# Constants and scalar parameters of a gate stage moved into the stage before it, and its first products reordered

## The reference

```python
# per head and chunk of 32: T = inverse of a unit lower triangle, then
u = T @ (v * beta);  w = T @ (k * beta)
def step(S, (q_i, k_i, u_i, w_i)):                   # over the chunks
    attn = where(incl_lower, q_i @ k_i.T, 0)
    u_adj = u_i - w_i @ S
    o_i = q_i @ S + attn @ u_adj
    S = S + k_i.T @ u_adj
local_short = fir(v, 3 taps);  local_long = fir(v, 63 taps)
stats = [mean, var, mean |x|, l2 norm] of local_short, local_long, delta_out, v
logits = gelu([hs, stats] @ gW1 + gb1) @ gW2 + gb2
probs = softmax(logits / exp(log_temp))
floor = 0.05 * sigmoid(floor_param)
probs = probs * (1 - sum(floor)) + floor
o = probs[0] * local_short + probs[1] * local_long + probs[2] * delta_out + probs[3] * v
o = o + sigmoid(conv_res_logit) * local_short + alpha_id * (hs @ Wid)
o = rms_norm(o) * o_norm_w;  out = o @ Wo             # then norm and routing to one of 8 experts
```

## Time and profile before

| | |
|---|---|
| Time, median of 3 runs | 1134.49 us (1133.34 to 1134.78) |
| The profiled execution's own time | 1135.28 us |
| Its span, first to last instruction | 1133.1 us |
| Mean granted clock of PE | 0.873 |
| PE busy | 909.3 us (80%) |
| DVE busy | 739.6 us (65%) |
| ACT busy | 556.5 us (49%) |
| POOL busy | 459.8 us (41%) |
| Inverse stage, from PE's first transposes | 678.0 us on |
| Gate stage, opening | 744.7 to 789 us |
| Gate stage, loop | 789 to about 1006 us |

### The profile page before, as it was taken

One profiled execution on the slowest core, in us unless ns is written; L12 is line 12 of the kernel. 1 busy time (PEld: TensorE's weight loads), 2 busy tenths in 40 slices (PEclk: granted clock), 3 DMA queues, 4 the chain that ended last, 5 costly groups with the idle time before them and its releaser, 6 DMA issues. The chain is left out here.

```text
span 1133.1 us, 34126 instructions
## 1 busy us (share of the span) xinstructions
PE 909.3 (80%) x12733; PEld 648.5 (57%) x12734; DVE 739.6 (65%) x2236; ACT 556.5 (49%) x1120; POOL 459.8 (41%) x590
## 2 busy tenths in 40 slices
PE   5899999999724999992788979479998996308995
PEld 2466666676613998992344447366555542307884
DVE  3558888888452555551488888913788888624664
ACT  1466766666311555551566753154455545206773
POOL 1001333444462444442477620021135555544776
PEclk8799999999656999997799979767999888658998
DMA  2011211245012222213333230131112151011210
GB/s 89 20 40 48 58 39 49 59 124 160 23 42 62 61 60 56 56 54 95 83 89 86 43 117 39 75 108 53 49 54 64 59 197 39 19 38 47 53 54 21
DMA packets 122117, 73.15 MB, mean 65 GB/s; under 512 B 63363, under 2 KB 108521, under 8 KB 121600
## 3 DMA queue, kind: packets, MB, share of 16 engines
q1 hardware_dynamic: 115328, 58.59, 18.9%
q0 software_dynamic: 6656, 12.70, 3.5%
HBM read 42.69 MB, written 27.51 MB: 62 GB/s over the span
## 5 line engine op out<-in xcount | busy, mean ns | idle before, releaser
L1129 ACT ACTIVATE bx_h<-bx_up,bx_cur 128x128 f32<-128x128 f32 x288 | 82.1, 368 | 104.4 <-PE bx_up L1100 104.4
L577 POOL DMA_INDIRECT regions_b<-a_xo,a_seat x64 | 63.7, 996 | 132.7 <-DVE a_seat L872 115.6
L1058 POOL DMA_INDIRECT chosen_b<-bx_ys,bx_to x72 | 76.1, 1057 | 90.6 <-DVE bx_ys L1172 87.7
L683 ACT ACTIVATE a_at<-a_scores 128x1024 f32<-128x1024 f32 x64 | 65.7, 1026 | 62.3 <-PE a_scores L451 61.8
L1100 PE MATMUL bx_up<-bx_xT,bx_cur 128*128 128x128 f32 x576 | 82.8, 288 | 2.0 <-DVE bx_cur L1145 0.6
L1082 PE MATMUL bx_down<-bk_w,bx_h 128*128 x576 | 82.1, 286 | 0.4 <-ACT bx_h L1129 0.4
L1100 PEld LDWEIGHTS bx_up<-bx_xT,bx_cur 128*128 128x128 f32 x576 | 71.4, 195 | 11.1 <-DVE bx_cur L1145 4.9
L1082 PEld LDWEIGHTS bx_down<-bk_w,bx_h 128*128 128x128 f32 x576 | 69.9, 192 | 3.9 <-issue 0.6
L1145 DVE TENSOR_SCALAR bx_cur<-bk_w 128x516 f32 x72 | 30.9, 429 | 58.5 <-issue 55.8
L1329 PE MATMUL c_bank<-c_xT,c_wc 128*128 128x512 f32 x128 | 63.7, 644 | 6.6 <-DVE keep_attn L1521 5.8
L446 PE MATMUL a_scores<-a_rk,a_kx 32*128 32x128 f32 (+3 forms) x1024 | 59.9, 300 | 7.0 <-DVE a_kx L750 4.1
(11 more groups left out here) (431 smaller groups left out, 2447.4 us busy)
## 6 DMA issues: line engine op xcount, KB each, us to landing
bx_xs<-regions_b SPq DMA_DIRECT2D x72, 65.0 KB, 1.8
bk_w<-in_b_w SPq DMA_DIRECT2D x16, 256.0 KB, 5.5
c_part<-chosen_b SPq DMA_DIRECT2D x16, 256.0 KB, 4.0
space<-in_d_w SPq DMA_DIRECT2D x16, 256.0 KB, 5.3
dx_xs<-regions_d SPq DMA_DIRECT2D x40, 65.0 KB, 1.8
a_xp<-in_a_xT SPq DMA_DIRECT2D x8, 256.0 KB, 3.3
a_xr<-in_x SPq DMA_DIRECT2D x8, 256.0 KB
lion_values<-a_vt SPq DMA_DIRECT2D x8, 256.0 KB, 2.4
```

The costliest lines, as they stand in the source:

```text
L577: nc.gpsimd.indirect_dma_start(route["regions"], bass.IndirectOffsetOnAxis(ap=seat[b][:, k, t:t + 1], axis=0), xo[b][k][:, t, :], None).th ...
L683: op(at[m % 2][:], S4[:, :, 0:320].rearrange("p g (q k) -> p g q k", q=2)[:, :, :, 0:P], ACT.Copy).then_inc(s_ata, 1)
L1058: nc.gpsimd.indirect_dma_start(dest, bass.IndirectOffsetOnAxis(ap=to[u][:, 0:1], axis=0), ys[u][:], None, bounds_check=dest.shape[0] - 1, ...
L1129: i = op(h[u % 2][:, f, :], BU[u % 2][:, f * P:(f + 1) * P], act_fn, bias=cur[u % 2][:, FC * P + f:FC * P + f + 1])
```

## The change

The new function `gate_tables` allocates the gate stage's tables and parameters outside both stages, so that they live through the delta stage too. `delta_invert` gets the list of 17 loads and issues them on SP as its first work, ahead of the wait for the filter's copies; and ACT, behind its last copy of the filter, waits for them all and makes the two sigmoids and the exponential. In the gate stage SP begins with the first rows. DVE begins with the small steps on parameters and makes the transitions of chunk 1 and the pad column behind them. PE turns the scaled output weights right behind the products of chunk 0, does the first wide product ahead of the transitions of chunk 1 and the second behind them, and the additions of chunk 1 in one piece. ACT copies the turned weights behind the first kept state.

```diff
@@ delta_invert (the inverse stage), SP and ACT
+            for dst, src in loads:
+                sp.dma_start(dst, src).then_inc(s_later, 16)
             sp.wait_ge(s_fc, 8)
             sp.dma_start(l_rows, fir[:].rearrange("p m c -> p (m c)")).then_inc(s_out, 16)
...
+            act.wait_ge(s_later, 16 * len(loads))
+            op(later["floor"][:], later["fpar"][:], ACT.Sigmoid)
+            op(later["res"][:], later["crl"][:], ACT.Sigmoid)
+            nc.scalar.preload_act_table_set("natural_log_exp_and_others")
+            op(later["itc"][:], later["temp"][:], ACT.Exp, scale=-1.0)
             U = keep["A"][:].rearrange("p n s c -> p c (n s)")
@@ new: gate_tables allocates the tables and lists their loads, before both stages
+def gate_tables(nc, ctx, w, consts, route):
+    where, columns = constant_columns("chunk_token", "ident")
...
+    loads = [(con[:], consts[:, columns]), (t["eye32"][:], consts[:, constant_columns("eye32", "eye32")[1]]),
+             (t["fpar"][:], w["floor"]), (t["crl"][:], w["crl"]), (t["temp"][:], w["temp"]),
+             (t["g1"][:], w["g1"]), (t["g1s"][:], w["g1s"]), (t["gb1"][:], w["gb1"]), (t["gw2"][:], w["gw2"]),
+             (t["wid"][:], w["wid"]), (t["wox"][:, 0:P], w["wo"]), (t["onw"][:], w["onw"]), (t["gbias"][:], w["gbias"]),
+             (t["alpha"][:], bc(w["alpha"], 4)), (t["gb"][:], bc(route["gate_b"], NE)),
+             (t["ident_gate"][:, P:P + NE], route["gate_w"]),
+             (t["ident_gate"][:, 0:P], consts[:, constant_columns("ident", "ident")[1]])]
+    return t, loads
@@ gate_stage, SP
-            sp.dma_start(eye32[:], eye).then_inc(s_in, 16)
...
-            for dst, src in loads:
-                sp.dma_start(dst, src).then_inc(s_w, 16)
             for m in range(2):
                 load_branches(m)
                 load_x(m)
@@ gate_stage, PE
             w_and_u(0, 0)
             w_and_u(0, 1)
+            pe.wait_ge(s_pv, 1)
+            nc.tensor.transpose(S[:, 0:P], wox[:, 0:P], C["ident"]).then_inc(s_wg, 1)
             additions(0)
             w_and_u(1, 0)
             w_and_u(1, 1)
+            hidden_state(0, 0)
             transition(1, 0)
             transition(1, 1)
-            pe.wait_ge(s_w, NW)
-            pe.wait_ge(s_pv, 1)
-            nc.tensor.transpose(S[:, 0:P], wox[:, 0:P], C["ident"]).then_inc(s_wg, 1)
-            additions(1, 0, 8)
-            hidden_state(0, 0)
-            additions(1, 8, 16)
             hidden_state(0, 1)
+            additions(1)
             pe.wait_ge(s_wgc, 1)
@@ gate_stage, ACT
             keep_state(0)
+            act.wait_ge(s_wg, 1)
+            op(won[:], S[:, 0:P], ACT.Copy).then_inc(s_wgc, 1)
             copy_wu(1, 0)
             copy_wu(1, 1)
-            act.wait_ge(s_w, NW)
-            op(floor[:], fpar[:], ACT.Sigmoid).then_inc(s_pa, 1)
-            op(res[:], crl[:], ACT.Sigmoid).then_inc(s_pa, 1)
-            nc.scalar.preload_act_table_set("natural_log_exp_and_others")
-            op(itc[:], temp[:], ACT.Exp, scale=-1.0).then_inc(s_pa, 1)
             act.wait_ge(s_set, 11)
-            act.wait_ge(s_wg, 1)
-            op(won[:], S[:, 0:P], ACT.Copy).then_inc(s_wgc, 1)
             square(0)
@@ gate_stage, DVE
-            dve.wait_ge(s_in, 16)
-            transitions(1, 0)
-            transitions(1, 1)
-            dve.wait_ge(s_w, NW)
-            dve.wait_ge(s_set, 11)
-            dve.wait_ge(s_pa, 3)
             own.restart(dve)
-            v.tensor_scalar(pad[:, P:P + 1], C["row"], float(SKIP), None, ALU.add).then_inc(s_padr, 1)
             v.tensor_copy(run[:], C["region"])
...
             dve.wait_ge(s_pv, 1)
+            transitions(1, 0)
+            transitions(1, 1)
+            dve.wait_ge(s_set, 11)
+            v.tensor_scalar(pad[:, P:P + 1], C["row"], float(SKIP), None, ALU.add).then_inc(s_padr, 1)
@@ gate_stage, POOL
-            pool.wait_ge(s_w, NW)
             then(op.tensor_copy(tok[:], C["chunk_token"]))
```

More of the change, by code:

```diff
@@ L1591, in _, with delta_invert @@
             dve.wait_ge(s_keep, 5 * NG)
-def delta_invert(nc, sem, keep, l_rows, w, consts):
+def delta_invert(nc, sem, keep, l_rows, later, loads):
     NB, LAGS = TOK // 32, 3
@@ L2541, in _, with delta_stage @@
             top_sums(NG - 1)
-def delta_stage(nc, sem, held, x_parts, xT_rows, l_rows, v_rows, s_rows, w, consts):
+def delta_stage(nc, sem, held, x_parts, xT_rows, l_rows, v_rows, s_rows, later, loads, w, consts):
     with ExitStack() as ctx:
@@ L2551, in delta_stage @@
         delta_project(nc, sem, keep, x_parts, xT_rows, v_rows, s_rows, w, consts)
-        delta_invert(nc, sem, keep, l_rows, w, consts)
+        delta_invert(nc, sem, keep, l_rows, later, loads)
 def host_layout(inp):
@@ L2669, in block_program @@
             held["kv"] = space[:, TOK:].rearrange("p (n k s c) -> p n k s c", n=NCH, k=2, c=32)
[L2670 to L2671 removed]
+            later, loads = gate_tables(nc, inner, pick("c"), ins["consts"], route)
+            stage(delta_stage, held, [x1, chosen[0:TOK], chosen[TOK:]], xT_rows, l_rows, v_rows, s_rows, later, loads,
+                  pick("c"), ins["consts"])
+            stage(gate_stage, held, l_rows, v_rows, s_rows, xT_rows, later, route)
         stage(expert_stage, "d", regions_d, out, route, keep, NT_TOP1, ACT.Gelu, ins["consts"], True)
```

49 lines of the change are left out of this document (15 added, 34 removed).

## The result

The changed kernel takes 1132.16 us (median of 12 runs, 1129.39 to 1134.37) against 1135.94 us of before in the same job (12 runs, 1133.34 to 1137.93). The ratio is 0.9969 with a 95% interval of 0.9956 to 0.9981: faster by 3.5 us (2.2 to 5.0). The direction was forecast, the size was not: 6.1 us was said, and the interval excludes it. (The median of before was 1134.49 us in its first three runs; against that the gain is 2.3 us.)

The account below looks back on a forecast made before the run. The gate stage's opening was taken as a chain of latencies: turned statistics at 768.3 instead of 774.86 gain 6.6 us, less 0.5 for the clock, 6.1 carried whole through the loop; forecast 1128.4 us, range 1126.0 to 1132.3.

Parts of the forecast that it names:

- Loads and parameters, cost 0: Inverse stage: 17 loads, sigmoids, exponential and table loads fit ACT's 14.5 us wait, at no cost.
- State rows land at +13.2: Gate-stage opening: state copies land at 758, between bounds 757.6 and 761.4.
- rival B: Gate-stage opening: state rows land late, at 761.4; gain 4.3 us, total 1130.2 us; chance 0.12.
- The turned weights inside PE's wait: Behind the second half of PE's first products: turning fits a 0.75 us wait; at most 0.2 us shows.
- DVE's sums of squares at +16.2: Gate-stage opening: DVE's sums start at 761.0 rather than 765.84 and end at 768.2.
- Carried products, as the additions, 2.1: 765.7.: End of PE's chunk 1 work: carried products take 2.1 us, ending at 765.7 instead of 774.9.
- I take 0.5 lost: Behind the turned statistics: uncertain clock costs 0.5 us, reducing the 6.6 us gain to 6.1.
- rival D: Gate-stage opening: 2.5 us of new PE idling drops the clock; slower, 1137.5 us; chance 0.05.
- Rival A: Half clock throughout the gate-stage opening; gain 3.0 us, total 1131.5 us; chance 0.16.
- rival C: Loop behind the opening: the gain vanishes downstream; total within 2 us of 1134.5; chance 0.05.
- The forecast case: Main prediction for the whole kernel: 6.1 us gained, 1128.4 us, own gain range 3 to 8.5 us; chance 0.62.

Follow-up runs that it names:

- e6: Changed kernel, but SP issues rows and x of chunk 1 only after chunk 1's carried products; gate-stage opening 37.5 us, one run.
- e10: Same program as e6, now timed; gate-stage opening 40.1 us, ratio to before 0.9941.
- e5: The kernel before the change, profiled once more without edit; gate-stage opening 43.2 us.
- e11: The changed kernel again without edit, in the same job as e9; gate-stage opening 39.7 us, ratio to before 0.9967.
- e2: Changed kernel with rows and x of chunk 1 issued right behind chunk 0's, ahead of the first state copies; opening 39.9 us, ratio to before 0.9978.
- e3: Changed kernel with PE's order and ACT's copy of the turned weights as before; gate-stage opening 44.6 us, ratio to before 0.9933.
- e12: e3 with the late chunk 1 rows of e6; gate-stage opening 40.1 us, one run.
- e13: Changed kernel, chunk 1 rows late, wide products among additions, half of chunk 2's w-and-u products and ACT's table load early; opening 38.9 us, ratio to before 0.994.
- e14: e13 once more; gate-stage opening 39.9 us, one run.
- e9: Changed kernel with chunk 1 rows late as in e6 and ACT's gelu table loaded early; opening 37.2 us, ratio to before 0.9936.

## Why the prediction was wrong in size

The moves did what they were made for, up to the second wide product. What failed is the stretch behind it, in which PE was to be done early and wait for DVE: PE ended last again. In the sum two terms were mis-sized.

- **Loads and parameters, cost 0.** Right: done by 727, 11.36 us of ACT's wait left.
- **State rows land at +13.2.** Right: ACT was released at +13.6; rival B's late landing did not happen.
- **The turned weights inside PE's wait.** Right: 0.35 us of that wait was left, and the first additions began at +4.4 as before. DVE's steps took 2.9 us and not 2, which this wait hid.
- **DVE's sums of squares at +16.2.** Right: +15.7, statistics ready at +22.8.
- **"Carried products, as the additions, 2.1: 765.7."** This failed. From the start of the additions of chunk 1 to the end of the carried products I had 4.7 us (761.0 to 765.7); it took 9.0 (763.16 to 772.2). 1.60 is the stop, which I had no term for, and about 2.6 is the clock falling in the middle: additions, gate products and carried products at 1.2 GHz. I had PE ready 2.6 us ahead of DVE; either loss would have fitted into that, both together did not. The turned statistics started at +24.9, not at +23.5. 1.4 us of the missing 2.5. Removing the rows from that stretch gave just this back (+23.4 and +23.7 in e6 and e10), with the clock falling all the same.
- **"I take 0.5 lost" for the clock behind them.** It cost 1.6: 15.8 us from the turned statistics to the loop's first step, against 14.2 before. The clock came back only at +32.6, as late as in before, though everything stood 5 us earlier. The other 1.1 us. I had weighed rival D's fall of the clock and given it 0.05 as a whole; half of it came, 7.7 us at half clock behind the turned statistics instead of 15, and not by the idling that I named, for there was none. Its premise is weak too: in e5 3.42 us of such idling left the clock full for another 1.4 us. In equal kernels the return came at +26.0 and +32.7 (e6, e10) or at +29.3, +32.6 and +33.0 (the changed one), which moved the stretch behind the turned statistics by 1.5 to 2.2 us, and I should have put that spread in. So the split of the missing 2.5 us holds for the first profile: in e11 the turned statistics came 1.9 us late and the stretch behind them took 14.3. What makes the clock fall and return when it does is not shown.
- **Rival A** did not come: the clock rose at +12.0 to +12.7 in 15 of the 16 profiles, and at +15.6 in e2. But it fell again at +19, under the additions and the carried products that A has at half clock.
- **The loop** carried the gain whole (344.1 and 344.2 us), against rival C.

The forecast case had 3 to 8.5 us as its range, and the measured 3.5 lies at its edge. The sum had PE at full clock and without a stop through the whole stretch, its good end.

## What to carry to other kernels

A gain computed from an engine's queue at full clock needs two more checks: whether that engine can be supplied with instructions at that pace while big transfers run, and whether the clock stays up over the stretch. An idle time that a change removes may have been hiding something else, here a late fetch. A gap marked "issue" inside a group of equal products is the sign of the first; look where it falls relative to the transfers and to the instruction packets of the DMA view, and count the records between two such gaps. Time transfers that nobody waits for (here the rows of chunk 1, needed 20 us later) behind the stretch in which the engine is critical. Here that moved the turned statistics by a microsecond or more; in the whole time it was not clear of noise. And where a clock's return scatters between runs of one kernel, read stages from several profiles before trusting a microsecond.

## What the runs showed of the hardware

- PE stops at places 127 to 128 products apart in its program, for 0.2 to 3.1 us, without a semaphore: in the new order 0.97 to 1.97 us with the rows under way (340 GB/s at 763 in the changed kernel), and at most 0.4 in all at the same place without them. In the old order there were 3.08 us with the rows and still 0.93 to 1.71 without (e3, e12, e13, e14), so traffic is a cause and not the only one. At half clock they were rarer but not absent (1.16 us in e2).
- Each of these stops ended 2.2 to 2.6 us (once 2.9) after a packet of the instruction queue began, with rows under way or without. With rows the packet ahead of the additions of chunk 1 began at +15.0 to +16.4, without them at +13.0 to +14.6.
- The granted clock rose at +12.0 to +12.7 in 15 of 16 profiles and fell at +18.8 to +19.6 in eleven of them, behind 3.42 us of idling and more work (e5), behind a stop (the changed kernel) or behind work without a gap (e6, e9, e10). The Trainium skill (TensorE: Matmul & The Clock Gate, Part 1: The HAM clock gate) ties the clock to how busy PE has been. In e6 PE worked without a gap from +4.4 to +19.3 and the clock fell at +19.2, so by these rows PE's busy time alone does not tell it. With the wide products among the additions and the same late rows (e12) it fell 3.5 us later. The return came between +26.0 and +36.6, and differed by 6.7 us between two profiles of one program (e6, e10).
- DVE's scalings of 128 x 128 took 0.52 to 0.59 us beside POOL's copies, instead of 0.28 to 0.29 us alone before: the small steps took 2.9 us instead of 1.8. It hid behind PE's first products.
